# An expert tile on TensorE waits for the landed results of the fourth tile back

## The chip, the cores and the metric

The kernel runs on one core of a Trainium2 chip. The metric is device time in microseconds of one execution; the median of several runs is given, and one further execution was profiled. The engines are PE (TensorE), DVE (VectorE), ACT (ScalarE), Pool (GpSimd) and SP (SyncE, which here issues plain DMAs). Each runs its own list of instructions in order; they meet on semaphores.

## What is computed

One post-norm transformer layer on 8 sequences of 512 tokens with 128 features: causal attention with 16 heads, then a mixture of 14 experts of which each token uses two. Cut to what matters:

```python
x = layernorm(x + attention(x))              # (8, 512, 128), 16 heads of 8, causal
probs = softmax(x @ gate_w.T)                # 14 experts
top2_p, top2_i = top_k(probs, 2)
w = top2_p / max(top2_p.sum(-1), 1e-10)
all_out = gelu(x @ w1[e] + b1[e]) @ w2[e] + b2[e]    # 128 -> 256 -> 128, per expert e
moe_out = w[:, 0:1] * out_of_first + w[:, 1:2] * out_of_second
x = layernorm(x + clip(x + moe_out, -100, 100))
```

## The kernel before

The first 340 us are attention, sequence by sequence. Every token's row (128 features and an id) is written twice into xs_dram, once for each of its experts, at a place within that expert's region; Pool does this with indirect DMAs (send, L722). The experts then work on tiles of 128 such rows, 77 tiles (NT), numbered in the order of a table that names each tile's expert and first row. Tables come in two parts: the first covers tiles 0 to 31 (FULL), the second, finished after the last sequence, the rest.

A tile j passes through these stations:
- SP loads its rows from xs_dram into slot j % 16 of xs (load_tiles, L487, 66 KB). From tile 16 on it first waits until the results of tile j-16 have landed (L486), since slot and id are still in use until then.
- DVE copies the expert's weights into slot j % 4 of w_cur (L1531).
- PE turns the tile (L1144, a transpose by matmul), ACT copies it from psum to xsT (L880), PE multiplies by the first weights (L1154), ACT applies gelu (L889), PE multiplies by the second weights (L1173), DVE adds the bias into slot j % 16 of y_sb (L1524).
- Pool writes the 128 result rows by an indirect DMA to their places in o_dram (put_out, L730). Its landing raises y_scattered[j % 16] by 16. The rows' ids are read from xs.

PE's code for this is a function step(j), which in one go turns tile j, does the first matmuls of tile j-1 and the second matmuls of tile j-2. Steps 0 to 11 are placed by hand between the last work of attention (TAIL["pe"]); steps 12 (TAIL_STEPS["pe"]) to 78 run in a plain loop (L1204), with the turn of the second table (L1106) ahead of step 13. DVE's step(j) adds the bias of tile j-4 and then copies the weights of tile j; ACT's step(j) copies the turned tile j, then does the gelu of tile j-1, and from step 14 on also makes one diagonal matrix of routing weights per step (L901) for the final stage.

Pool's list of work is fixed too: the scatters of tiles 0 to 3 (OUT_AHEAD), then small operations for the last sequence, tiles 4 to 8 (OUT_FIRST), then the eight send scatters of the last sequence, then tiles 9 to 76. Once a step ahead stands in its list and waits, everything behind it waits too.

After the last tile, PE sums the inputs of the last norm into psum (L1221), SP waits for all of y_scattered (L557) and loads the results from o_dram (L562), PE adds them weighted by the diagonals (L1230), DVE clips and takes statistics, Pool and ACT finish the norm (L755, L915), SP stores (L567).

Of the kernel before, what the change touches and what calls it, by code (L numbers as in the profile page):

```python
# [14 lines left out]
def post_ln_attention_moe(nc, x, xT, WqT, bq, WkT, bk, WvT, bv, WoT, bo, gateT, w1, b1T, w2, b2, out):  # L15
# [25 lines left out]
    STEP = 16  # L41
# [19 lines left out]
    with ExitStack() as ctx:  # L61
# [3 lines left out]
        def sem(name):  # L65
            return ctx.enter_context(nc.semaphore(name))
# [170 lines left out]
        y_scattered = [sem(f"y_scattered_{r}") for r in range(STEP)]  # L237
# [58 lines left out]
        def live(b):  # L296

            return 0 <= b < B
# [51 lines left out]
        def y_bank(j):  # L350

            return psum[:, 4 + (j % 2 if j < FULL else j % 4), 0:D]
# [14 lines left out]
        TAIL_STEPS = {"pe": 12, "act": 12, "dve": 13}  # L367
        TABLE_STEP = 13
        TAKE_STEP = 16
        OUT_AHEAD = 4  # L370
        OUT_FIRST = 9

        FIRST_STEPS = 16
# [3 lines left out]
        def tile_live(j, count=NT):  # L377
            return 0 <= j < count
# [20 lines left out]
        def _(sp):  # L399
# [81 lines left out]
            def load_tiles(first, end):  # L481
                for j in range(first, end):
                    if (j - first) % LOOK == 0:
                        found = lookup(mybir.EngineType.SP, 1, DUMP, j)
                    if j >= STEP:
                        sp.wait_ge(y_scattered[j % STEP], 16 * (j // STEP))  # L486
                    sp.dma_start(xs[:, j % STEP, :], xs_dram[bass.ds(found[(j - first) % LOOK], P), :]  # L487
                                 ).then_inc(xs_loaded[j % STEP], 16)
# [53 lines left out]

            load_tiles(STEP, STEP + OUT_FIRST)

# [3 lines left out]
            sp.dma_start(xs_dram[DUMP:DUMP + P, :], pad[:]).then_inc(S["padded"], 16)  # L548
            load_tiles(STEP + OUT_FIRST, FULL)
            sp.wait_ge(S["padded"], 16 * (E + 1))  # L550
# [37 lines left out]
        def _(pool):  # L588
# [60 lines left out]
            def body(b, odd):  # L649
                for c in range(NG):  # L650
# [22 lines left out]
                    if c == 0 and b == B:  # L673
                        put_out(0, OUT_AHEAD)
                    if c == 1 and not live(b) and live(b - 1):
# [3 lines left out]
                    if c == 2 and b == B:  # L679
                        put_out(OUT_AHEAD, OUT_FIRST)  # L680
                    if c == 3 and b == B:
# [44 lines left out]
            def put_out(first, end):  # L726
                for j in range(first, end):
                    u = j % STEP
                    pool.wait_ge(S["y_copied"], j + 1)
                    pool.indirect_dma_start(  # L730
                        o_dram, bass.IndirectOffsetOnAxis(xs[:, u, D:D + 1].bitcast(I32), 0), y_sb[:, u, :], None,
                        bounds_check=TOPK * NTOK - 1, oob_is_err=False).then_inc(y_scattered[u], 16)

            batches(body)

            put_out(OUT_FIRST, NT)

# [184 lines left out]
        def _(pe):  # L922
# [139 lines left out]
            def body(b, odd):  # L1062
                for c in range(NG):
# [10 lines left out]
                    for k in range(NBANK):  # L1074
                        if live(b):
                            score_bank(b, c, k)
                        if k == M_AT and live(ahead(b, c, 1)[0]):
                            turn_maxima(*ahead(b, c, 1))
                        if k in UNIT_AT and live(sb_):
                            score_unit(sb_, sc_, UNIT_AT[k])  # L1080
                        if k in PV_AT and live(pb_):
                            pv(pb_, pc_, PV_AT[k])
                        if (b, c) == (0, 2) and k in FOLD_AT:
                            fold(FOLD_AT[k])
                        if b == B:
                            for j in TAIL["pe"].get((c, k), ()):
                                step(j)
                        if closing(b) and (c, k) == TABLE_AT[2]:
                            turn_table(0)
                        if (c, k) in misc_of(b) and not (waiting and misc_of(b)[c, k] == "k"):  # L1090
                            shared(b, c, k, misc_of(b)[c, k], odd)
                        for name in ("q", "k"):
                            for n in (1, 2):
                                if MISC.get((c, k - PART_STEP * n)) == name:
                                    ob = owner(b, c, name)[0]
                                    if live(ob) and not (ob == 0):
                                        take_off(ob, name, n, ps_m)
# [36 lines left out]
            def step(j):  # L1134
                if tile_live(j):
                    r = j % STEP
                    pe.wait_ge(xs_loaded[r], 16 * (j // STEP + 1))
                    if j >= 2:
                        pe.wait_ge(S["xsT_copied"], j - 1)
                    else:  # L1140

                        pe.wait_ge(S["s_reduced"], NUNIT * NG * B)
                        pe.wait_ge(S["experts_loaded"], 16 * 5)
                    pe.transpose(psum[:, r % 2, 0:P], xs[:, r, 0:D], ident[:]).then_inc(S["xsT_filled"], 1)  # L1144
                j -= 1
                if tile_live(j):

                    u = j % STEP
                    pe.wait_ge(S["xsT_copied"], j + 1)
                    pe.wait_ge(S["w_copied"], j + 1)  # L1150
                    if j >= 2:
                        pe.wait_ge(S["gelu_done"], j - 1)
                    for ch in range(FC):
                        last = pe.matmul(psum[:, 2 + u % 2, P * ch:P * ch + P], w_cur[:, u % WR, P * ch:P * ch + P],  # L1154
                                         xsT[:, u % 2, :], start=True, stop=True)
                    last.then_inc(S["h_filled"], 1)
                j -= 1
                if tile_live(j):

                    u = j % STEP  # L1160
                    pe.wait_ge(S["gelu_done"], j + 1)
                    if j < 2:
                        pe.wait_ge(S["exp_done"], NBANK * NG * B)
                    elif j < FULL + 2:
                        pe.wait_ge(S["y_copied"], j - 1)
                    elif j == FULL + 2:
                        pe.wait_ge(drained["ot"], NG * B)
                    elif j == FULL + 3:
                        pe.wait_ge(S["tables_ready"], 2)
                    if j >= FULL + 4:  # L1170
                        pe.wait_ge(S["y_copied"], j - 3)
                    for ch in range(FC):
                        last = pe.matmul(y_bank(j), hT_sb[:, u % 2, P * ch:P * ch + P],  # L1173
                                         w_cur[:, u % WR, W2_AT + P * ch:W2_AT + P * ch + D],
                                         start=(ch == 0), stop=(ch == FC - 1))
                    last.then_inc(S["y_filled"], 1)
# [27 lines left out]
            for j in range(TAIL_STEPS["pe"], NT + LAG):  # L1204
                if j == TABLE_STEP:
                    turn_table(1)
                step(j)
# [480 lines left out]
```

## Time and profile before

| | us |
|---|---|
| median of 3 runs | 504.43 (503.44 to 506.19) |
| profiled execution | 503.98 |
| span of its profile | 502.1 |
| mean granted PE clock in it | 0.974 |

The span is from the first to the last instruction; 1.9 us lie around it. Times in the rows are microseconds from the span's start. PE is TensorE's matmul side, PEld its loading of weights, which overlaps. "Granted clock" is the share of full speed that the chip let TensorE have: 1.00 is 2.4 GHz and 0.50 is 1.2 GHz. Instructions that only wait, branch or issue a DMA don't count as busy. An indirect DMA of Pool does occupy it, as DMA_INDIRECT.

### The profile page before, as it was taken

Reading aid. Unit: us, or ns where it says so; the run is one execution under the profiler, and the core shown is the slowest. Engines: PE = TensorE matmul, PEld = TensorE weight load, DVE = VectorE, ACT = ScalarE, POOL = GpSimd, SP = SyncE. Lnnn points to the kernel's source line nnn. Section 1 sums busy time; section 2 is a strip of 40 time slices with the busy share of each in tenths; the row PEclk is TensorE's granted clock in tenths of the full one; section 3 lists DMA queues with packets and bytes.
Section 4 is the critical chain, followed back from the end, with each engine's and each line's share of the span. In section 5 each row is a group of like instructions: output and inputs, shape, how many; then the busy total and the mean of one; then the engine's idle time right before and its main releaser. Section 6 shows DMA issues by size and latency. Waiting matters only on the chain.

```text
span 502.1 us, 11159 instructions
## 1 busy us (share of the span) xinstructions
PE 428.1 (85%) x3556; PEld 268.9 (54%) x3589; DVE 394.6 (79%) x975; ACT 331.0 (66%) x809; POOL 282.5 (56%) x455
## 2 busy tenths in 40 slices
PE   5789999999999999999999989978879898884970
PEld 2354455445446445445445544525768778774870
DVE  6987879988988998898898899877887676550291
ACT  4285676876866776777686675675678888780054
POOL 6022334245834835645664574678777777777173
PEclk9999999999999999999999999999889999997896
DMA  5647397434343445254244332014254333321563
GB/s 165 196 159 204 107 293 226 144 123 143 117 147 117 119 141 163 83 178 150 88 150 131 119 93 65 28 50 125 58 146 121 100 101 92 87 82 32 187 208 108
DMA packets 74392, 64.58 MB, mean 129 GB/s; under 512 B 9030, under 2 KB 68685, under 8 KB 74336
## 3 DMA queue, kind: packets, MB, share of 16 engines
q1 hardware_dynamic: 68528, 55.08, 36.6%
q0 software_dynamic: 4512, 8.54, 5.2%
q8 instruction: 29, 0.48, 0.4%
q10 hardware_dynamic: 1296, 0.27, 0.3%
q14 instruction: 27, 0.22, 0.2%
HBM read 36.88 MB, written 25.46 MB: 124 GB/s over the span
## 4 chain that ended last, share of the span: by engine, by line
PE 36%; DVE 33%; DMA 9%; issue 9%; POOL 5%; ACT 5%; SPq 1%; ACTq 1%; DVEq 0%; another core or an unknown queue 0%; POOLq 0%
DVE nmax L1313 17%; PE psum L986 9%; PE psum L945 6%; PE psum L968 6%; POOL o_dram L730 3%; DMA experts<-o_dram 3%; DMA o_dram<-probs,xs 3%; PE psum L1007 3%; PE psum L953 3%; DVE ov L1321 3%; DVE w_cur L1531 2%; DMA xs<-xs_dram 2%; PE psum L1014 2%; PE psum L1173 2%; PE psum L1154 2%
## 5 line engine op out<-in xcount | busy, mean ns | idle before, releaser
L779 ACT ACTIVATE probs<-psum 128x512 f32<-128x512 f32 x320 | 180.1, 596 | 81.2 <-PE psum L968 47.7
L1313 DVE TENSOR_REDUCE nmax<-psum 128x2 f32<-128x1024 f32 (+3 forms) x224 | 196.3, 911 | 23.8 <-PE psum L953 23.3
L663 POOL TENSOR_SCALAR_AFFINE_SELECT probs<-probs 128x256 f32<-128x256 f32 (+1 forms) x192 | 87.8, 485 | 125.4 <-ACT probs L779 124.7
L945 PE MATMUL psum<-kst,qst 128*128 128x512 bf16 (+2 forms) x511 | 109.5, 299 | 6.4 <-DVE nmax L1313 5.6
L968 PE MATMUL psum<-qst,kst 128*128 128x128 bf16 (+3 forms) x480 | 101.0, 295 | 7.1 <-ACT probs L779 2.7
L730 POOL DMA_INDIRECT o_dram<-probs,xs x77 | 78.4, 1018 | 24.4 <-issue 18.6
L986 PE MATMUL psum<-probs,vst 128*32 128x512 f32 (+3 forms) x1024 | 82.2, 439 | 1.5 <-POOL probs L663 1.3
L953 PE MATMUL psum<-bmask,bident 128*128 128x256 bf16 (+1 forms) x320 | 80.3, 251 | 0.1
L968 PEld LDWEIGHTS psum<-qst,kst 128*128 128x128 bf16 x512 | 40.1, 98 | 53.7 <-ACT probs L779 33.1
L945 PEld LDWEIGHTS psum<-kst,qst 128*128 128x128 bf16 x512 | 47.2, 98 | 32.9 <-DVE nmax L1313 12.3
L889 ACT ACTIVATE hT_sb<-psum,w_cur 128x128 f32<-128x128 f32 x154 | 48.3, 364 | 7.7 <-PE psum L1154 6.8
L1531 DVE COPY w_cur<-experts 128x642 f32 x77 | 42.1, 550 | 12.1 <-DVE probs L1524 4.1
L1173 PE MATMUL psum<-w_cur,hT_sb 128*128 128x128 f32 x308 | 48.7, 282 | 3.1 <-DVE probs L1524 2.3
L1154 PE MATMUL psum<-xsT,w_cur 128*128 128x128 f32 x308 | 48.8, 282 | 0.0
L1173 PEld LDWEIGHTS psum<-w_cur,hT_sb 128*128 128x128 f32 x308 | 41.6, 196 | 4.0 <-issue 2.1
L1154 PEld LDWEIGHTS psum<-xsT,w_cur 128*128 128x128 f32 x308 | 41.9, 197 | 0.2
L986 PEld LDWEIGHTS psum<-probs,vst 128*32 128x32 f32 x1024 | 25.4, 109 | 30.2 <-issue 24.1
L953 PEld LDWEIGHTS psum<-bmask,bident 128*128 128x128 bf16 x320 | 31.3, 98 | 12.6 <-issue 0.2
L1524 DVE TENSOR_TENSOR probs<-psum,w_cur 128x128 f32<-128x128 f32 x77 | 22.2, 288 | 19.9 <-PE psum L1173 18.3
L915 ACT ACTIVATE xr<-xr,fin_off,fin_rs 128x128 f32<-128x128 f32 x32 | 12.6, 479 | 32.6 <-POOL fin_off L758 32.6
L1144 PE MATMUL psum<-ident,xs 128*128 128x128 f32 x77 | 23.8, 309 | 10.6 <-DMA xs<-xs_dram 7.8
L880 ACT ACTIVATE xsT<-psum 128x128 f32<-128x128 f32 x77 | 21.2, 276 | 16.3 <-PE psum L1144 16.0
(200 smaller groups left out, 557.4 us busy)
## 6 DMA issues: line engine op xcount, KB each, us to landing
kst<-dk SPq DMA_DIRECT2D x62, 128.0 KB, 2.8
qst<-dq SPq DMA_DIRECT2D x31, 256.0 KB, 3.1
xs<-xs_dram SPq DMA_DIRECT2D x77, 66.0 KB, 1.9
experts<-o_dram SPq DMA_DIRECT2D x7, 512.0 KB, 4.4
dk<-k SPq DMA_DIRECT2D x7, 384.0 KB, 2.6
dq<-q SPq DMA_DIRECT2D x7, 384.0 KB
xT_sb<-in_xT SPq DMA_DIRECT2D x8, 256.0 KB, 3.1
xTv_sb<-in_xT SPq DMA_DIRECT2D x8, 256.0 KB, 3.3
```

Of the source, the lines that this page charges most:

```text
L663: pool.affine_select(out=view, in_=view, compare_op=ALU.is_ge, fill=0.0, base=0, pattern=[[0, view.shape[1]], [1, P]], channel_multiplier= ...
L730: pool.indirect_dma_start(o_dram, bass.IndirectOffsetOnAxis(xs[:, u, D:D + 1].bitcast(I32), 0), y_sb[:, u, :], None, bounds_check=TOPK * N ...
L779: act.activation(probs[:, c % 2, p, kk * T:(kk + 1) * T], ps_t[:, k % 2, :], ACT.Exp, scale=SCALE).then_inc(S["exp_done"], 1)
L889: last = act.activation(hT_sb[:, u % 2, P * ch:P * ch + P], psum[:, 2 + u % 2, P * ch:P * ch + P], ACT.Gelu, bias=w_cur[:, u % WR, B1_AT + ...
L945: pe.matmul(bank[:, at:at + w], qst[:, c, e, P * i:P * i + P], kst[:, c, h, e, 0:w], start=(at == 0), stop=False, skip_group_check=True)
L953: pe.matmul(diag_blocks, bident[:], bmask[:, 0:diag_blocks.shape[1], :], start=False, stop=True, skip_group_check=True).then_inc(S["s_fill ...
L968: last = pe.matmul(ps_t[:, k % 2, at % T:at % T + w], kst[:, c, g % 2, pair, P * j:P * j + P], qst[:, c, pair, P * j:T], start=True, stop= ...
L986: last = pe.matmul(ps_o[32 * g:32 * g + 32, P * j:T], vst[:, j, 4 * c + g, :], probs[:, c % 2, g // 2, at:at + w], start=(j == 0), stop=(j ...
L1154: last = pe.matmul(psum[:, 2 + u % 2, P * ch:P * ch + P], w_cur[:, u % WR, P * ch:P * ch + P], xsT[:, u % 2, :], start=True, stop=True)
L1173: last = pe.matmul(y_bank(j), hT_sb[:, u % 2, P * ch:P * ch + P], w_cur[:, u % WR, W2_AT + P * ch:W2_AT + P * ch + D], start=(ch == 0), st ...
L1313: last = dve.tensor_reduce(o, i, AX.X, ALU.max, negate=True)
L1531: dve.tensor_copy(w_cur[:, j % WR, :], experts[:].rearrange("p e f -> p (e f)")[:, bass.ds(found[j // LOOK][j % LOOK], WCOLS)]).then_inc(S ...
```

## The change

PE's step(j) gets one more wait ahead of the turn of tile j, for every tile from 12 on: the semaphore y_scattered of tile j-4 must have reached its count, so the results of tile j-4 have landed in o_dram. Step 12 is the first step of the plain loop. Nothing else is changed.

```diff
         OUT_AHEAD = 4
+        PACE = 4
+        PACE_FROM = TAIL_STEPS["pe"]
         OUT_FIRST = 9
...
                 if tile_live(j):
                     r = j % STEP
                     pe.wait_ge(xs_loaded[r], 16 * (j // STEP + 1))
+                    if j >= PACE_FROM:
+
+                        behind = j - PACE
+                        pe.wait_ge(y_scattered[behind % STEP], 16 * (behind // STEP + 1))
                     if j >= 2:
                         pe.wait_ge(S["xsT_copied"], j - 1)
```

## Rows read from the trace of the kernel before

**Rows 1.** The page: busy time of each engine, share of the span, instructions.

```profile
PE 428.1 (85%) x3556; PEld 268.9 (54%) x3589; DVE 394.6 (79%) x975; ACT 331.0 (66%) x809; POOL 282.5 (56%) x455
```

**Rows 2.** Waits from 378 to 452 us: total us, times, longest.

```profile
PEld psum L1144 <- DMA xs<-xs_dram: 14.2, 22, 2.1
POOL o_dram L730 <- issue: 13.7, 45, 0.3
POOL o_dram L730 <- DVE probs L1524: 3.7, 12, 0.3
```

**Rows 3.** Timeline of Pool (start, us): tiles 8, 9, 10, 16, 76.

```profile
363.66 0.97 POOL L730 DMA_INDIRECT o_dram<-probs,xs  x1 [0.30 <-issue]
...
376.21 1.24 POOL L730 DMA_INDIRECT o_dram<-probs,xs  x1 [0.30 <-DVE probs L1524]
377.76 0.97 POOL L730 DMA_INDIRECT o_dram<-probs,xs  x1 [0.30 <-issue]
...
385.57 1.05 POOL L730 DMA_INDIRECT o_dram<-probs,xs  x1 [0.30 <-issue]
...
464.68 0.97 POOL L730 DMA_INDIRECT o_dram<-probs,xs  x1 [0.30 <-issue]
```

**Rows 4.** Timeline of PE and DVE: steps 13, 16, 20, 73 and 76.

```profile
367.26 0.42 PE L1144 MATMUL psum<-ident,xs 128*128 128x128 f32 x1
...
368.33 1.06 PE L1173 MATMUL psum<-w_cur,hT_sb 128*128 128x128 f32 x4
...
372.34 0.27 PE L1144 MATMUL psum<-ident,xs 128*128 128x128 f32 x1
...
376.39 0.27 PE L1144 MATMUL psum<-ident,xs 128*128 128x128 f32 x1
...
444.61 0.33 PE L1144 MATMUL psum<-ident,xs 128*128 128x128 f32 x1 [0.90 <-DMA xs<-xs_dram]
...
445.88 0.29 DVE L1524 TENSOR_TENSOR probs<-psum,w_cur 128x128 f32<-128x128 f32 x1 [1.21 <-PE psum L1173]
...
449.26 0.27 PE L1144 MATMUL psum<-ident,xs 128*128 128x128 f32 x1
...
452.34 0.29 DVE L1524 TENSOR_TENSOR probs<-psum,w_cur 128x128 f32<-128x128 f32 x1 [0.60 <-PE psum L1173]
```

**Rows 5.** Timeline, then chain that ended last: tile 1's add and scatter.

```profile
349.91 0.25 DVE L1524 TENSOR_TENSOR probs<-psum,w_cur 128x128 f32<-128x128 f32 x1
350.95 0.98 POOL L730 DMA_INDIRECT o_dram<-probs,xs  x1 [0.82 <-DVE probs L1524]
...
350.23 0.73 issue
352.81 1.02 issue
```

**Rows 6.** Landings of L730 (all; 364 to 378), then stretches: length, PE, PEld, DVE, ACT, POOL busy, PEclk.

```profile
DMA to landing us min/median/max: 2.1/2.3/3.9
DMA to landing us min/median/max: 2.5/2.5/2.7
356.20:359.60 3.40, 1.67 (x13) 1.34 (x12) 2.46 (x11) 1.51 (x6) 2.55 (x7) 1.00 0.02 5
359.60:363.00 3.40, 3.40 (x26) 3.36 (x27) 3.00 (x14) 3.35 (x10) 2.79 (x3) 0.51 0.26 78
429.80:433.20 3.40, 1.50 (x14) 1.31 (x13) 1.47 (x4) 1.61 (x7) 2.49 (x4) 1.00 0.27 65
463.80:467.20 3.40, 3.40 (x17) 3.18 (x17) 0.00 (x0) 0.00 (x0) 1.55 (x2) 0.50 0.02 0
```

**Rows 7.** End of the expert stage: chain that ended last, and PE's next group.

```profile
464.68 2.08 DMA o_dram<-probs,xs
467.02 2.69 DMA experts<-o_dram
466.80 2.86 PEld L1221 LDWEIGHTS psum<-xr,ident 128*128 128x128 f32 x16 [0.22 <-DMA o_dram<-probs,xs]
```

## The prediction

> **What bounds the kernel now.** I read the page first: PE is busy for 85% of the span, but that is a mean over attention and experts [rows 1]. The change touches the expert tiles alone, so I went to the waits of the stretch from 378 us to 452 us, where PE runs its steady loop over tiles. There Pool idles only 17.4 us in 57 pieces of about 0.30 us, nearly all of them put down to issue or a short wait for DVE, while PE waits for xs loads [rows 2]. Pool's order of time shows the same: the scatter of tile 9 starts at 376.21, that of tile 76 at 464.68, so 67 scatters in 88.47 us, 1.32 us each; undisturbed they follow at 1.28 us, 0.97 busy and 0.30 between [rows 3]. PE alone needs about 1.01 us a tile (tiles 16 to 20, turned from 372.34 to 376.39, four steps) [rows 4]. So Pool sets the pace, and PE runs ahead of it until the ring of 16 rows in xs is full; its waits for xs loads are this ring. How far ahead is seen from two rows: PE turns tile 20 at 376.39, and Pool only starts the scatter of tile 16 at 385.57 [rows 3, 4]. PE's last tile is turned at 449.26, its result is added by DVE at 452.34, and Pool needs until 464.68 to work off the backlog. Its last scatter lands at 466.76, and the results are loaded from 467.02 on; nothing of the final stage can go before that [rows 4, 7].
>
> **The change, part by part.** It adds one PE wait to each of tiles 12 to 76, 65 in all. A satisfied semaphore wait costs next to nothing on PE (no row of L1144 shows it apart from the 0.1 us between its pieces), so the instruction is put at 0. No DMA, copy or matmul is added or moved. What counts is when the wait passes. Tile j may be turned only after tile j-4 has landed; by the two rows for tiles 20 and 16 that is over 11 us later than now, so the wait binds.
>
> Queued behind the waiting instruction are all of step j: the turn of tile j, the first matmuls of tile j-1 and the second matmuls of tile j-2. DVE's add of j-2 and Pool's scatter of j-2 wait for these. So step j waits for the landing of j-4, whose second matmuls were in step j-2: a loop over two steps, not four. Its length, piece by piece:
> - From the turn in step j-2 to the add of tile j-4: 1.27 us at full clock (444.61 to 445.88, a step with all its inputs ready) [rows 4].
> - The add: 0.29 us [rows 4].
> - From the add's end to the scatter's start with Pool idle. Before, Pool almost always has a queue, which hides this. The one clear case is tile 1: the add ends at 350.16, the scatter starts at 350.95, 0.79 us. The chain gives 0.73 us of it to issue, and 1.02 us in another case, where Pool was still busy at first [rows 5]. Bounds 0.73 and 1.02; I take 0.79, the case nearest to an idle Pool.
> - Scatter's start to landing: 2.1 least, 2.3 median, 3.9 most; 2.5 in the stretch after 364 us [rows 3, 6]. I take 2.3, since the xs loads of 66 KB still fall between the scatters, with 2.1 and 2.5 as bounds.
> - Landing to PE's start: 466.76 to 466.80 before the last group of L1221, so 0.05 [rows 7].
> Sum: 1.27 + 0.29 + 0.79 + 2.3 + 0.05 = 4.70 us for two tiles, 2.35 us a tile against 1.32 now. Even and odd tiles are two such loops side by side. Their PE work (two steps of about 1.01) and Pool work (2 x 1.28) fit into 4.70, so neither engine stretches them.
>
> On the landing the Trainium skill (DMA: Bandwidth & Descriptors, Latency and other measured facts) speaks for the change: lighter HBM load makes the fixed cost smaller. By it the landing would go to the 2.1 of the quiet end of the trace, 31 x 0.2 = 6 us less in the sum; the trace has 2.08 us for the last, undisturbed scatter against the 2.3 median, so it agrees in direction.
>
> The clock of PE is the second term. In the loop PE works some 2.1 of 4.7 us, 45%. The stretches show both answers for such a share: after 1.67 us busy of 3.40 (356.2 to 359.6) the granted clock is 0.51, half; 1.50 us busy (429.8 to 433.2) left it at 1.00. At half clock PE was then fully busy for one such stretch (359.6 to 363.0), and at another place (463.8 to 467.2) it was fully busy and the clock still 0.50 [rows 6]. At half clock the step costs 1.27 + 0.86: the turn starts at 367.26, the last matmuls at 368.33 end at 369.39, 2.13 us [rows 4]. That makes the loop 5.56 us, with PE busy 3.9 of it, a share at which the clock would often come back. With nothing that decides between them I take the middle, 5.13 us.
>
> The Trainium skill (TensorE: Matmul & The Clock Gate, What's actually happening) says that idleness throttles PE and activity releases it. If the gaps of the loop counted as idle throughout, its result would be the half-clock case below.
>
> Start of the loops. Tile 12 waits for tile 8 (scatter at 363.66, landed about 366.2), hidden, because step 13 comes after the second table and so turns its tile only at 367.26 anyway [rows 3, 4]. Step 13 waits for tile 9. Its scatter stands on Pool's queue behind the eight L722 scatters of the last batch and starts at 376.21; landed and seen, 376.21 + 2.5 + 0.05 = 378.8, where tile 13 is now turned at 367.26. Tile 14 follows tile 10: 377.76 + 2.55 = 380.3 [rows 3, 4]. DVE's take_table(1) moves behind the add of tile 11 to about 380.5; SP needs that table only for tile 32, hidden.
>
> End. Tile 76 is 31 loops after tile 14: 380.3 + 31 x 5.13 = 539.3. Steps 77 and 78 have no wait; from the turn of tile 76 to its add is 3.08 us now (449.26 to 452.34), up to 1.6 more at half clock, 0.8 taken. Then 0.29 + 0.79 + 2.08. So the last landing is at 539.3 + 3.1 + 0.8 + 3.1 = 546.3, against 466.76: 79.6 us later. Two savings are already in this: Pool's backlog of 12.3 us after 452.34 is gone, and so are PE's waits for xs loads. The final stage (loads of o_dram, sum, norm, stores) stays as it is; PE's first matmuls on xr end in part before the landing as now. Diagonals on ACT run one a step and stay hidden.
>
> **The sum.** The profiled execution takes 503.98 us with a span of 502.1, 0.45 under the median of 504.43. 503.98 + 79.6 = 583.6; I give 583.
>
> **The rivals.**
> - Full clock throughout. For it: 1.50 us busy of 3.40 without a fall. Loop 4.70: tile 76 at 526.0, last landing 6.24 later at 532.3, +65.5, so 569.
> - Half clock throughout. For it: the fall after 1.67 busy, and the half clock that stays beside a busy PE from 463.8 to 467.2. Loop 5.56: tile 76 at 552.7, landing at 560.5, +93.7, so 598.
> - Pool hides it, faster than before. If a loop took no more than two of Pool's intervals, 2.56 us, the wait would only take away PE's useless lead, Pool would stay at the bound, and the crowded scatters (tile 9: 1.24 busy) would fall to the undisturbed 1.28 spacing: 67 x (1.32 - 1.28) = 2.7 us gained, 501. Its point of decision is the landing: 2.1 us of it alone leave under 0.5 us for matmuls, add and Pool's start, so it needs a tile's results to be counted as landed much earlier than the rows say.
> - The change does not do what it says: the semaphore's count passes early, and nothing changes, 504. Against it: SP's own xs loads wait on the same semaphores with the same count, and PE is seen waiting for them.
>
> **How the numbers follow.** Mixed clock 0.45, full clock 0.27, half clock 0.23, Pool hides it 0.02, no effect 0.03. For the range: shortest loop 1.27 + 0.29 + 0.73 + 2.1 + 0.05 = 4.44, which gives 561; longest 2.13 + 0.29 + 1.02 + 2.5 + 0.05 = 5.99, which gives 611. All extremes at once are unlikely at the upper end, so 560 to 604. About 0.5%, 2.5 us, is what a measurement of this kernel can tell from no change. Faster 0.02, same 0.03, slower 0.95.
>
> **What would show it.** PE's turns come in pairs about 1.3 to 2 us apart, then a gap, with the wait put down to the DMA into o_dram; the releaser xs<-xs_dram disappears. L1144's 65 starts from tile 12 spread over some 160 us instead of 87. Pool's idle before L730 rises from 0.30 to over 1 us, mostly after DVE. The granted clock in the stage says which of the first three cases it is. The first long stall is before tile 13. The final stage keeps its 35 us from first load to end. I am wrong if Pool's scatters still follow at 1.3 us, if an idle Pool starts its scatter at 0.3 us after the add (then 31 x 0.5 = 15 us less), or if landings drift to 3 us and more.

## The result and the profile after

The changed kernel takes 597.2 us (median of 4, 595.85 to 598.74) where the kernel before takes 505.31 beside it: ratio 1.183, interval 1.180 to 1.186. It is 92 us slower. The forecast was 583 with a range of 560 to 604.

The page of the changed kernel: span and busy time, and the granted PE clock in 40 slices of the span (tenths of full speed). They answer to [rows 1].

```profile
span 595.5 us, 11192 instructions
PE 478.7 (80%) x3589; PEld 307.8 (52%) x3589; DVE 392.0 (66%) x975; ACT 337.6 (57%) x809; POOL 278.8 (47%) x455
PEclk9999999999999999999999997687666665567896
```

DVE, ACT and Pool have the same work as before, in a span that is 93 us longer. PE is busy 51 us longer with the same instructions, because from the 25th slice on its clock is well below full. Over the stretch of the paced loop (length, PE, PEld, DVE, ACT, Pool busy, granted clock, DMA share, GB/s) it is 0.66:

```profile
380.00:561.00 181.00, 126.37 (x624) 113.61 (x623) 50.21 (x129) 76.44 (x257) 64.13 (x66) 0.66 0.15 39
```

The waits of the changed kernel from 378 to 550 us (total us, times, longest), which answer to [rows 2]:

```profile
DVE probs L1530 <- PE psum L1179: 119.6, 62, 9.1
POOL o_dram L732 <- DVE probs L1530: 106.5, 56, 3.7
PEld psum L1150 <- issue: 75.5, 55, 10.1
```

(L1530, L732, L1150, L1160 and L1179 are the former L1524, L730, L1144, L1154 and L1173.) The waits for xs loads are gone. PE waits ahead of the turn. The prediction expected this wait to be put down to the DMA into o_dram; the trace does not name its releaser ("issue"), so that it is the landing is seen from the times alone: in the median a turn comes 0.09 us after the landing of the fourth tile back. Pool, which had 0.30 us between its scatters, now waits for DVE 56 times, almost 2 us each.

The loop in the timeline of the changed kernel. The first two rows are the turns of tiles 13 and 14, then come the adds and scatters of tiles 22 and 23 and the turns of tiles 26 and 27. They answer to [rows 3, 4].

```profile
378.54 0.44 PE L1150 MATMUL psum<-ident,xs 128*128 128x128 f32 x1 [9.62 <-issue]
380.50 0.42 PE L1150 MATMUL psum<-ident,xs 128*128 128x128 f32 x1
...
408.71 0.29 DVE L1530 TENSOR_TENSOR probs<-psum,w_cur 128x128 f32<-128x128 f32 x1 [1.96 <-PE psum L1179]
409.77 0.97 POOL L732 DMA_INDIRECT o_dram<-probs,xs  x1 [1.91 <-DVE probs L1530]
410.94 0.29 DVE L1530 TENSOR_TENSOR probs<-psum,w_cur 128x128 f32<-128x128 f32 x1 [1.31 <-PE psum L1179]
412.00 0.97 POOL L732 DMA_INDIRECT o_dram<-probs,xs  x1 [1.26 <-DVE probs L1530]
413.21 0.45 PE L1150 MATMUL psum<-ident,xs 128*128 128x128 f32 x1 [2.31 <-issue]
415.17 0.42 PE L1150 MATMUL psum<-ident,xs 128*128 128x128 f32 x1
```

From an add's end to its scatter's start it is 0.77 us here (409.00 to 409.77) and 0.77 or 0.78 in 61 of the 65 cases from tile 12 on. From the scatter at 409.77 to the turn at 413.21 it is 3.44 us; this is one of the few late ones, and the median is 2.34. Tile 76 is turned at 552.12; from tile 14 that is 171.6 us for 62 tiles, 2.77 us each. The stage's end in the chain that ended last, answering to [rows 7]:

```profile
552.12 0.45 PE psum L1150
...
558.20 2.08 DMA o_dram<-probs,xs
...
560.55 2.73 DMA experts<-o_dram
```

The last landing is at 560.28 against 466.76 before, 93.5 us later. From there to the end it is 35.3 us, as before. All of the loss lies in the expert stage.

### The profile page after: what moved, and what is told of

It is laid out like the page before. It is cut to its first block, busy times and chain, and to the rows that moved or that the text cites. A ratio compares the mean times of both kernels' runs of the same rounds, so it can differ in the third digit from the quotient of the medians.

```text
span 595.5 us, 11192 instructions
## 1 busy us (share of the span) xinstructions
PE 478.7 (80%) x3589; PEld 307.8 (52%) x3589; DVE 392.0 (66%) x975; ACT 337.6 (57%) x809; POOL 278.8 (47%) x455
## 4 chain that ended last, share of the span: by engine, by line
PE 48%; DVE 24%; issue 16%; ACT 4%; DMA 4%; POOL 2%; ACTq 0%; SPq 0%; DVEq 0%; POOLq 0%
DVE nmax L1319 14%; PE psum L1160 9%; PE psum L1179 8%; PE psum L988 8%; PE psum L970 6%; PE psum L947 5%; PE psum L1150 4%; DMA experts<-o_dram 3%; PE psum L1009 2%; PE psum L955 2%; DVE ov L1327 2%; PE psum L1016 2%; ACT xr L917 1%; DVE onT_sb L1337 1%; ACT q L793 1%
## 5 line engine op out<-in xcount | busy, mean ns | idle before, releaser
L732 POOL DMA_INDIRECT o_dram<-probs,xs x77 | 75.4, 980 | 121.2 <-DVE probs L1530 111.9
L947 PE MATMUL psum<-kst,qst 128*128 128x384 bf16 (+3 forms) x512 | 109.8, 299 | 6.4 <-DVE nmax L1319 5.6
L970 PE MATMUL psum<-qst,kst 128*128 128x512 bf16 (+3 forms) x512 | 108.6, 301 | 3.9 <-ACT probs L781 2.6
L1530 DVE TENSOR_TENSOR probs<-psum,w_cur 128x128 f32<-128x128 f32 x77 | 22.4, 290 | 126.7 <-PE psum L1179 126.6
L1150 PE MATMUL psum<-ident,xs 128*128 128x128 f32 x77 | 30.1, 391 | 68.4 <-issue 67.2
L1160 PE MATMUL psum<-xsT,w_cur 128*128 128x128 f32 x308 | 72.0, 378 | 0.0
L1179 PE MATMUL psum<-w_cur,hT_sb 128*128 128x128 f32 x308 | 68.0, 363 | 3.0 <-DVE probs L1530 2.2
L1179 PEld LDWEIGHTS psum<-w_cur,hT_sb 128*128 128x128 f32 x308 | 61.5, 278 | 3.8 <-issue 2.0
L1160 PEld LDWEIGHTS psum<-xsT,w_cur 128*128 128x128 f32 x308 | 61.3, 279 | 0.4 <-ACT xsT L882 0.2
L1150 PEld LDWEIGHTS psum<-ident,xs 128*128 128x128 f32 x77 | 13.1, 170 | 83.2 <-issue 81.7
L1537 DVE COPY w_cur<-experts 128x642 f32 x77 | 38.3, 500 | 11.9 <-DVE probs L1530 4.0
```

What stands on the lines that cost most here:

```text
L732: pool.indirect_dma_start(o_dram, bass.IndirectOffsetOnAxis(xs[:, u, D:D + 1].bitcast(I32), 0), y_sb[:, u, :], None, bounds_check=TOPK * N ...
L947: pe.matmul(bank[:, at:at + w], qst[:, c, e, P * i:P * i + P], kst[:, c, h, e, 0:w], start=(at == 0), stop=False, skip_group_check=True)
L970: last = pe.matmul(ps_t[:, k % 2, at % T:at % T + w], kst[:, c, g % 2, pair, P * j:P * j + P], qst[:, c, pair, P * j:T], start=True, stop= ...
```

## The experiments

The runs were made in three groups, each on a chip of its own, and in each the kernel before ran beside them. In the first group it took 533.45 us; in the second and third 505.55 and 505.27. Ratios are within a group. Three kernels of the first group were therefore run again on the third chip; e2_behind was not, and the changed kernel itself was not run on the first chip.

### The same kernels in a second trace

> The kernel before, unchanged, to have its trace from the chip on which the experiments ran, where it takes some 533 us and not 505. Theory (that chip is slower in the loads of xs or in the landings, not in PE, DVE or Pool's own work): the scatters take 0.97 to 1.3 us as before, the attention part ends within 1% of the first chip, and the 28 us more lie in the expert stage as waits for DMAs. Rival (Pool's work per scatter is slower): the scatters follow at 1.6 us or more without idle time of Pool. If the chip of this run is the first one, the time is 505 and the point stays open.

Measured: 506.03 us, so the slower chip was not met again and the point stays open. The trace confirms the first one: 1.30 us a tile, scatters at 1.33 us, last scatter at 466.87.

> The changed kernel, unchanged, beside the other runs of this call. Theory: its loop of two tiles is set by the step, the add, Pool's start and the landing, none of which goes by the chip, so 5.4 to 5.7 us again and a time near 597 to 610 also where the kernel before takes 533; the ratio then shrinks from 1.18 to 1.12 to 1.14. Rival (a slower chip slows both alike): 1.18 x 533 = 630.

Measured: 599.43 us, ratio 1.182 (1.175 to 1.189), 2.75 us a tile. On this chip the question of a slower chip couldn't be asked; the size of the loss repeats.

### How many steps the loop covers

```diff
-        PACE = 4
+        PACE = 5
```

> The changed kernel with the wait on the fifth tile back (PACE 5). Theory (the loop covers PACE - 2 steps): 4.7 us at full clock to 5.56 at half for three tiles, 1.57 to 1.85 us a tile, against 2.77 measured with PACE 4; expert stage 62 x (2.77 - 1.75) = 60 us shorter, time 535 to 550. Rival (time goes by tiles under way, latency over PACE: 2.77 x 4 / 5 = 2.2 us a tile): 35 us shorter, time 560 to 570.

Measured: 531.41 us, ratio 1.052 (1.046 to 1.059), 1.71 us a tile (380.61 to 486.73 for 62 tiles). One tile more in flight takes 1.04 us off each tile. Three steps at 1.71 make 5.1 us, between the 4.70 and 5.56 of the prediction; the rival's 2.2 us a tile is excluded. The time is 4 us under the forecast of 535 to 550; the clock, which that forecast left open, held at 0.97. PE's stretch in this kernel and in the changed one (length, PE, PEld, DVE, ACT, POOL busy, clock, DMA share, GB/s), this kernel first:

```profile
385.00:465.00 80.00, 58.69 (x424) 52.66 (x424) 38.90 (x95) 53.13 (x188) 45.64 (x47) 0.97 0.29 74
```

```profile
385.00:465.00 80.00, 54.28 (x266) 48.37 (x264) 22.99 (x59) 35.44 (x119) 28.21 (x29) 0.67 0.18 48
```

PE issues 424 matmuls here against 266, at nearly full clock.

> The changed kernel with the wait on the sixth tile back (PACE 6). Theory (the loop covers PACE - 2 steps): 4.70 us for four tiles is 1.18 us a tile, under Pool's 1.28, so Pool is the bound again and the time is 502 to 508, with the tiles under way at 6 or fewer. Rival A (loop counts all six): the same. Rival B (PE falls to half clock here too): 5.56 / 4 = 1.39 us a tile, time 508 to 515.

> The kernel of e4_pace6 again (wait on the landing of the sixth tile back), on another chip. Theory (four steps a loop, 4.7 / 4 = 1.18 us a tile at full clock, under Pool's 1.28): 505 to 512, a little above the kernel before, since PACE 5 measured 1.71 us a tile where 1.57 was the shortest loop, and the start of the stage (tile 15 waits for tile 9, behind the eight scatters of the last batch) costs up to 3 us. Rival (latency over tiles under way, 2.77 x 4 / 6 = 1.85 us a tile, as in the trace of e4_pace6): 535.

Measured: ratio 1.001 (0.998 to 1.003) in the first group, where both take 534; in the third 509.32 us, ratio 1.010 (1.007 to 1.014). The second is the clearer one: a loss of 4 us, small but clear of the noise. Pool is nearly the bound again: its scatters follow at 1.37 us against 1.32 before, with ten gaps longer than the usual 0.30 us that add 5.4 us. The rival's 535 is excluded on this chip. The time would also fit rival B of the first expectation (508 to 515), but its condition isn't met: the granted clock from 385 to 465 us is 1.00.

> The changed kernel with the wait on the landing of the eighth tile back (PACE 8). Theory: six steps a loop, 0.8 to 0.93 us a tile, far under Pool's 1.28; PE still runs ahead of Pool, only by less; time 503 to 506, not to be told from the kernel before. Rival (a shorter lead spares Pool the meetings with DVE's copies, scatters of 1.24 us fall to 0.97): 67 x 0.04 = 3 us faster, 501 to 503.

Measured: 504.45 us, ratio 0.9985 (0.9964 to 1.0006), no difference. The trace shows a part of the rival's mechanism: scatters follow at 1.30 us and take 0.99 us in the mean against 1.33 and 1.02 in e5_before. From tile 9 to tile 76 that is 87.0 us against 88.9. A gain of 1.5 to 2 us in the trace is not told apart in the times.

### What is in the loop

```diff
-                        pe.wait_ge(y_scattered[behind % STEP], 16 * (behind // STEP + 1))
+                        pe.wait_ge(S["y_copied"], behind + 1)
```

> The changed kernel, but PE waits for DVE's add of tile j-4 (y_copied) in place of its landing in DRAM. Theory (the cost is Pool's start, 0.78 us, plus the landing, 2.33 us, inside the loop): without them the loop is about 1.6 us for two tiles, below Pool's 2 x 1.28, the wait never binds, time 503 to 507. Rival (an extra wait ahead of the turn costs by itself, 65 times 0.1 us or more): 510 or more.

> The kernel of e3_copied again (the wait is on DVE's add of tile j-4 and not on its landing), on another chip. Theory (the cost is Pool's start and the landing inside the loop): PE runs ahead of Pool as before, Pool stays at 1.3 us a tile, time 503 to 507 where the kernel before takes 505. Rival (the wait as such costs, as the 1.86 us a tile in the trace of e3_copied might say): 520 or more.

Measured: ratio 0.9996 (0.997 to 1.002) in the first group, 1.001 (0.999 to 1.003) in the third, with 505.88 us. The same number of waits in the same place costs nothing once Pool's start and the landing are outside. The cost is in these two together, as was expected; no run takes out one without the other. PE is again 10 us ahead of Pool, and its waits are for the ring of xs as in [rows 2]; total, times and longest from 385 to 465 us:

```profile
DVE probs L1530 <- PE psum L1179: 16.0, 25, 1.5
POOL o_dram L732 <- issue: 12.8, 42, 0.3
PEld psum L1150 <- DMA xs<-xs_dram: 12.5, 20, 1.4
```

### What is queued behind the wait

Two kernels change only the order within PE's steps from 12 on (and ACT's: gelu ahead of the copy). The first:

```diff
+                if j < PACE_FROM:
+                    turn(j)
+                    first(j - 1)
+                    second(j - 2)
+                else:
+                    second(j - 2)
+                    first(j - 1)
+                    turn(j)
```

> The changed kernel, but from step 12 on PE does the second matmuls of tile j-2 and the first of j-1 ahead of the wait and the turn of tile j (ACT's order turned likewise: gelu, then copy). The wait is the same, on tile j-4. Theory (the cost comes from what is queued behind the wait): the results of tile j-4 now leave one step earlier, the loop covers three steps, about 0.95 + 0.29 + 0.78 + 2.33 = 4.4 us for three tiles, 1.45 to 1.6 us a tile; PE is busy some 70% and its clock mostly full; time 515 to 530. Rival (at most four tiles under way is the limit, whatever the order): four tiles stay under way and the time stays near 597.

Measured: 604.43 us beside 533.45, no gain. This misses my number, but it is not the rival either, because the landing has stopped binding: nearly every tile is turned 5.13 us after the scatter of the fourth tile back started, at even steps of 2.79 us, where a landing takes 2.2. The order made another chain. In its timeline the gelu waits for the first matmuls (L1170), the second matmuls (L1190) for the gelu, and the next first matmuls stand behind them:

```profile
454.96 1.06 PE L1170 MATMUL psum<-xsT,w_cur 128*128 128x128 f32 x4
...
456.06 0.63 ACT L892 ACTIVATE hT_sb<-psum,w_cur 128x128 f32<-128x128 f32 x2 [1.71 <-PE psum L1170]
...
456.74 1.22 PE L1190 MATMUL psum<-w_cur,hT_sb 128*128 128x128 f32 x4 [0.50 <-ACT hT_sb L892]
...
457.76 1.06 PE L1170 MATMUL psum<-xsT,w_cur 128*128 128x128 f32 x4
```

So the number failed on a chain that the expectation left out, and on the clock, which it had mostly full. It is 0.50 although PE is busy for 73.9 of 90 us:

```profile
390.00:480.00 90.00, 73.90 (x292) 61.06 (x292) 25.21 (x64) 34.71 (x129) 31.49 (x33) 0.50 0.19 50
```

The second order puts `first(j - 1)` ahead of `second(j - 2)`, so that a gelu has a whole step to finish.

> The changed kernel, but from step 12 on the first matmuls of tile j-1 and then the second of tile j-2 stand ahead of the wait and the turn of tile j (in the earlier attempt the second ones came first and waited for a gelu that had only just begun). The wait is the same, PACE 4. Theory (the cost is what is queued behind the wait): the results of tile j-4 leave one step earlier, the loop is about 1.7 + 0.29 + 0.78 + 2.33 = 5.1 us for three tiles, 1.7 us at full and 2.0 to 2.4 us at half clock; time 545 to 585. Rival (four under way is the limit in any order): 2.77 us a tile, the time of the changed kernel.

Measured: 548.4 us (four runs, 543.71 to 555.40; without the longest 548.1), ratio 1.088 (1.081 to 1.096), 1.89 us a tile, and the landing binds again (the turn comes 2.3 to 2.5 us after the scatter's start in most steps). With the same wait on the same fourth tile back, 51 us come back. A part of them is the clock, which is full here from 385 to 465 us:

```profile
385.00:465.00 80.00, 58.77 (x393) 46.35 (x391) 34.74 (x88) 50.30 (x175) 42.24 (x44) 1.00 0.25 68
```

The next experiment brings the clock back without a new order and takes 588 us, 40 us more than this one, at 2.57 us a tile. So what stands behind the wait, and not the number of tiles allowed in flight, sets most of the loss.

### The clock

```diff
+                if j + 2 >= PACE_FROM:
+                    for _ in range(WARM):      # WARM = 8
+                        pe.matmul(psum[:, (j + 3) % 2, 2 * P:4 * P], bident[:], bmask[:], start=True, stop=True)
```

> The changed kernel, with 8 bf16 matmuls of 256 columns added behind each PE step from 12 on, into a part of psum that nobody reads (extra work, about 0.9 us a step, which fits the gap of 2.6 us in each loop). Theory (loop of two steps, lengthened by the half clock): the granted clock of the expert stage goes from 0.66 to near 1.00, the step to its add from a mean of 1.96 us to 1.3, the loop from 5.54 to about 4.75 us; last landing near 534, time 572 (566 to 578). Rival (the clock is a bystander, the landing and Pool's start set the loop): the loop stays above 5.3 us, time 590 or more.

> The kernel of e1_warm again (8 extra bf16 matmuls behind each PE step from 12 on), because in that call the kernel before took 533 us and not 505, on a chip that seems slower in DMAs. Theory (half clock and landing both in the loop): with the clock near 1.00 the step to its add is 1.29 us, the loop 4.8 to 5.0 us for two tiles (some collisions of the extra matmuls with the other loop), time 570 to 580 against 597 to 599 for the changed kernel. Rival (the clock is a bystander): 590 or more where the kernel before takes 505.

Measured: 590.09 us in the first group, ratio 1.106 (1.103 to 1.109), and 588.29 in the third, ratio 1.165 (1.160 to 1.170). The clock did come back; the stretch of the third group's run:

```profile
385.00:465.00 80.00, 65.92 (x525) 56.66 (x524) 24.35 (x62) 36.68 (x124) 29.18 (x30) 0.97 0.19 50
```

The turn to the add falls from a mean of 1.96 us to 1.29, as expected, which is 31 x 0.67 = 21 us. But the time falls by only 9 to 11 us (597.2 and 599.4 against 588.3). The theory's 570 to 580 is missed. The rival's 590 is just met in the first group, but its loop of over 5.3 us is not: 5.06 and 5.14 us.

The rest is given back at three places of this trace. Many loops close in 4.70 us, what the prediction has at full clock (27 of 61 in 4.65 to 4.75), but from a scatter's start to the turn the mean is 2.73 us against 2.47, which is 31 x 0.26 = 8 us. A little over half of that are late landings (mean 2.49 against 2.34). The other part is time in which the tile had landed and PE was still in the step before, extra matmuls included. And the loops begin 3.8 us later: the extra matmuls of step 13, still at half clock, take 1.92 us and hold up the turn of tile 14 (384.27 here, 380.50 in the changed kernel):

```profile
382.56 1.92 PE L1186 MATMUL psum<-bmask,bident 128*128 128x256 bf16 x8
...
384.27 0.42 PE L1151 MATMUL psum<-ident,xs 128*128 128x128 f32 x1
```

A late landing in this run, the scatters of tiles 29 and 30 and the turns of tiles 32 and 33:

```profile
432.00 1.05 POOL L733 DMA_INDIRECT o_dram<-probs,xs  x1 [1.22 <-DVE probs L1534]
432.15 0.30 PE L1151 MATMUL psum<-ident,xs 128*128 128x128 f32 x1 [0.39 <-issue]
434.51 0.97 POOL L733 DMA_INDIRECT o_dram<-probs,xs  x1 [1.47 <-DVE probs L1534]
435.86 0.30 PE L1151 MATMUL psum<-ident,xs 128*128 128x128 f32 x1 [1.58 <-issue]
```

Tile 33 is turned 3.86 us after the scatter of tile 29 began. In that stretch a packet of the queue that brings PE's instructions falls (DMA queues from 432 to 436 us: packets, MB, share of 16 engines; then the landing):

```profile
q8 instruction: 1, 0.02, 1.7%
...
o_dram<-probs,xs POOLq DMA_INDIRECT x2, 3.0
```

The kernel with the extra matmuls has nine such packets from 385 to 548 us, the changed kernel five from 380 to 560. (That the queue brings PE's instructions is read from its count, which alone rises with the extra matmuls, from 29 to 34 in all.) From tile 16 on 16 turns come over 2.9 us after their scatter. Eight of them are late landings: their scatters started 1.0 to 1.4 us before a packet and landed after 3.1 to 4.3 us. Of the other eight, seven have a landing on record, in 2.1 to 2.3 us, and waited for PE to finish the step before; seven of the eight come right behind a late landing. Scatters with no packet within 3 us landed after 2.31 us in the mean and 2.70 at most.

The same holds for every trace with landings on record, that of the kernel before included. Of 34 scatters from tile 12 on that started 0.7 to 1.5 us before a packet, 33 took over 2.9 us, and of 401 without a packet within 3 us, 4 did. It is a coincidence in time, not a proof: no run moved a packet. By it the extra matmuls, as instructions, cost a part of what they win as warmth.

## Why the prediction was right, point by point

**The bound before** stands: Pool's scatters at 1.3 us, PE some 10 us ahead. Waiting for the add alone (e10_copied) leaves all of this in place and costs nothing.

**The loop of two steps** stands. PACE 4 and 5 give 2.77 and 1.71 us a tile, and at PACE 6 and 8 the scatters follow at 1.37 and 1.30 us, Pool's own pace. This goes with the steps in the loop, not with latency over tiles in flight; and the second reordering gains 51 us at PACE 4, and is still 40 us faster than the kernel with extra matmuls, whose clock is near full too.

**The pieces at full clock** were 1.27 + 0.29 + 0.79 + 2.35 = 4.70 us. The traces have 1.29, 0.29, 0.78 and 2.33 to 2.34 in most loops whose step ran at full clock. The single row of an idle Pool, tile 1 in [rows 5], was worth trusting; neither 0.73 nor 1.02 came up as the typical value.

**The start** was 378.8 and 380.3 for tiles 13 and 14, measured 378.54 and 380.50. The closeness has luck in it: in e6_after they are 380.88 and 382.84, because Pool comes to the scatter of tile 9 2.3 us later.

**The clock** is the term that was mis-sized. I took the middle between full and half clock, a step of 1.70 us; it was 1.96, with a granted clock of 0.66 from 380 to 561 us. That is 31 x 0.26 = 8 us of the 14 us by which the last landing came later than forecast (560.3 against 546.3). The step that failed is the one that took the middle: with PE busy 3.9 of 5.56 us at half clock, the clock "would often come back". It was back for only about a third of the time from 380 to 561 us, and in e2_behind, with PE busy 73.9 of 90 us, it stayed at 0.50. The rows I leaned on showed already that half clock can outlast a fully busy stretch [rows 6], and I gave this too little weight. The two traces of the changed kernel differ in it (0.67 and 0.78 from 385 to 465 us) while their times agree within 0.4%. The Trainium skill (TensorE: Matmul & The Clock Gate, HAM oscillation) describes this going back and forth where short work alternates with waits; the trace agrees in that, with both kinds of step side by side: some turns reach their add in 1.29 us, others in 2.21. The page's case has waits of some 3 to 5 us, though; here the longest pause of PE between the turns of tiles 14 and 76 is 2.49 us.

**The landings and what follows them** make another 4 us: the mean from scatter's start to turn is 2.47 us against 2.35. The landing itself was sized well, 2.34 in the mean against 2.3. From the landing to the turn it is 0.09 at best where I had 0.05 from a single row, and 0.13 in the mean, because some turns waited for the other loop's step on PE. By the Trainium skill's rule on lighter load (DMA: Bandwidth & Descriptors, Latency and other measured facts) the landing would have come down to 2.1. It moved that way by far less: from tile 9 on the median went from 2.28 to 2.25 us and the mean from 2.43 to 2.34, and the shortest was 2.1 before and after. Another 1.2 us lie in the last steps (8.2 us from the last turn to the last landing, 7.0 forecast).

**The rivals.** The half-clock case gave 598 and the median is 597.2, but it is right by coincidence: its loop of 5.56 us is the measured mean of 5.54, but that is made of a clock at half for two thirds of the time, of late landings and of turns that waited for PE. The full-clock case (569) would have needed 28 us less; the run with extra matmuls came only 9 us down, of 21 that the clock alone would give. Pool did not hide the loop at PACE 4, and does at 8. Its gain of 2.7 us was forecast from undisturbed scatters; at PACE 8 the trace shows about two of these and the times none.

## What to carry to other kernels

Before limiting how many tiles are in flight, write down the loop that the new wait closes: from the waiting instruction through all that is queued behind it to the event waited for, and count how many tiles that loop really covers. Here it covered two of four. And price the engine's slower state too: this loop with pauses ran at a clock of 0.66 (0.97 with the pauses filled), and half-clock matmuls made its step 2.21 us long in place of 1.29.

## What the runs showed of the hardware

- An idle Pool starts an indirect scatter 0.78 us after the result that it waits for is written (0.77 or 0.78 in 60 to 62 of 65 cases in each kernel that waits for the landing of the fourth tile back). With a queue in front of it this is hidden, and 0.30 us between scatters is all that shows.
- Indirect scatters land 2.1 to 2.3 us after their start as a rule. Those that started 0.7 to 1.5 us before a 16 KB packet of PE's instruction queue took 2.9 to 4.3 us, in the kernel before too. The kernel with more PE instructions has more of these packets, nine against five in the loop. That the packet is the cause is not shown.
- PE was held at half clock in one kernel (e2_behind, on the first chip) for 90 us on end, busy 82% of the time.
- On the first chip the kernel before took 533 us, and so did the two kernels there that let PE run ahead (1.86 and 1.82 us a tile), while the kernel with the extra matmuls took 590 there and 588 elsewhere. Its scatters landed in the same 2.25 us, in the median of those on record. In the four traces of that chip SP needs 13 to 16 us for 14 writes of empty rows into xs_dram (pad) that take 9 us in the kernel before elsewhere, and in that of e3_copied DVE and ACT wait at places for 2 to 3 us with an unknown releaser. What slows that chip is not settled: the kernel before was not traced there.
